# Fetching the first layer's slot tiles up to 22 ahead, and moving and spacing the gathers of batches 2 to 7

## What is computed

```python
x = x + cumsum(layernorm(x) @ W.T + bias)                 # within a row of 128
x = x + ffn(layernorm(x))
x = x + attention(layernorm(x))                           # 16 heads, window of 128
x = x + ffn(layernorm(x))

def ffn(x):                                               # 8 experts, the best 2 for each token
    xn = layernorm(x) * gamma + beta
    probs = softmax(xn @ router_w.T / 1.5)
    w, idx = top_k(probs, 2)
    h = silu(einsum('btd,edf->betf', xn, W1))
    y = einsum('betf,efd->betd', h, W2)
    return sum over the 2 chosen experts of w * y, + x
```

## Time and profile before

| | us |
|---|---|
| median of 3 runs | 991.28 |
| lowest, highest | 985.68, 997.75 |
| profiled execution, its own time | 1000.25 |
| profiled execution, span of the trace | 997.8 |
| PE busy | 693.9 (70%) |
| DVE busy | 612.3 (61%) |
| POOL busy | 434.2 (44%) |
| ACT busy | 408.3 (41%) |

### The profile page before, as it was taken

The page is one execution under the profiler, slowest core; times in us unless marked ns, Lnnn a source line. Parts: engine busy times, 40 slices in busy tenths (PEclk is TensorE's granted clock), DMA queues, the critical chain, the costliest instruction groups (busy, mean ns, idle before and its releaser), DMA issues.

```text
span 997.8 us, 30496 instructions
## 1 busy us (share of the span) xinstructions
PE 693.9 (70%) x11616; PEld 531.7 (53%) x11616; DVE 612.3 (61%) x1840; ACT 408.3 (41%) x691; POOL 434.2 (44%) x409
## 2 busy tenths in 40 slices
PE   3701767797667678887977888877586677566670
PEld 2501556675556554654645656655475556455560
DVE  7887887864444567555646655677669534354444
ACT  1370245353333334553735645645354334233340
POOL 6691573584655500203023000050576666665661
PEclk9655678999877799998999989957658988788986
DMA  7200012132212221111111201001021111233114
GB/s 220 68 27 5 23 35 70 47 68 57 62 51 82 71 78 33 55 60 29 58 46 51 60 20 42 6 15 31 17 67 39 43 44 38 64 84 97 54 37 136
DMA packets 62922, 54.60 MB, mean 55 GB/s; under 512 B 10129, under 2 KB 55954, under 8 KB 62778
## 3 DMA queue, kind: packets, MB, share of 16 engines
q1 hardware_dynamic: 53250, 33.12, 11.6%
q0 software_dynamic: 9536, 19.55, 7.8%
HBM read 31.79 MB, written 20.84 MB: 53 GB/s over the span
## 4 chain that ended last, share of the span: by engine, by line
PE 40%; DVE 27%; issue 11%; another core or an unknown queue 9%; DVEq 4%; ACT 4%; DMA 2%; POOL 1%; SPq 0%; ACTq 0%; POOLq 0%
PE stbank L1107 6%; PE bank L1210 4%; PE stbank L1094 3%; PE stbank L1096 3%; DVE zr L584 3%; PE sbank L1168 3%; DVE gl L765 2%; PE stbank L1194 2%; PE stbank L1108 2%; PE sbank L1163 2%; PE stbank L1095 2%; DVE xs L781 2%; DVE mx L823 2%; DVE ysb L755 2%
## 5 line engine op out<-in xcount | busy, mean ns | idle before, releaser
L478 POOL DMA_INDIRECT xg<-table,idx x156 | 159.1, 1020 | 170.0 <-PE sbank L1075 60.6
L901 ACT ACTIVATE g<-stbank 128x512 f32<-128x512 f32 x156 | 93.3, 598 | 324.0 <-PE stbank L1096 239.7
L1107 PE MATMUL stbank<-wff,gh 128*128 x624 | 142.6, 307 | 111.3 <-DVE ysb L755 75.8
L433 POOL TENSOR_TENSOR r<-ve,mhalf 128x4 f32<-128x4 f32 (+1 forms) x32 | 43.0, 1344 | 299.1 <-DVE ve L561 201.7
L823 DVE TENSOR_REDUCE mx<-sbank 128x2 f32<-128x320 f32 (+1 forms) x256 | 116.6, 472 | 79.7 <-PE sbank L1168 59.3
L1094 PE MATMUL stbank<-xT,wff 128*128 128x128 f16 x624 | 152.1, 250 | 17.5 <-issue 8.9
L755 DVE TENSOR_REDUCE ysb<-stbank 128x128 f32<-128x256 f32 x156 | 66.0, 423 | 155.5 <-remote 101.6
L1096 PE MATMUL stbank<-xT,wff 128*128 128x128 f16 x624 | 152.1, 250 | 0.5 <-issue 0.5
L1095 PE MATMUL stbank<-xT,wff 128*128 128x128 f16 x624 | 149.9, 247 | 1.1 <-issue 1.1
L948 ACT ACTIVATE pT<-stbank 128x1024 f32<-128x1024 f32 (+1 forms) x128 | 117.0, 915 | 76.8 <-PE stbank L1194 76.0
L1107 PEld LDWEIGHTS stbank<-wff,gh 128*128 128x128 f16 x624 | 67.5, 108 | 143.9 <-issue 126.5
(11 more groups left out here) (188 smaller groups left out, 1344.1 us busy)
## 6 DMA issues: line engine op xcount, KB each, us to landing
yslot<-ysb SPq DMA_DIRECT2D x78, 64.0 KB
table<-tb SPq DMA_DIRECT2D x16, 256.0 KB
cg<-ytab SPq DMA_DIRECT2D x16, 256.0 KB
qz<-dumps SPq DMA_DIRECT2D x96, 32.0 KB
kst<-dumps SPq DMA_DIRECT2D x96, 32.0 KB
xg<-table,idx POOLq DMA_INDIRECT x156
xs<-in_x SPq DMA_DIRECT2D x8, 256.0 KB, 4.6
qz<-in_w SPq DMA_DIRECT2D x1, 2048.0 KB, 10.2
```

Of the source, the lines that this page charges most:

```text
L478: g.indirect_dma_start(xg[:, i % G].rearrange("p a d -> p (a d)"), None, table[cc % 2], bass.IndirectOffsetOnAxis(ap=idx[:, cc % 2, t:t + ...
L901: a.activation(g32[:, i % 3, :], hbank[i % 2], ACT.Silu, scale=1.0 / WSCALE)
L1107: mm(o, gh[:, i % 3, P * f:P * f + P], whl, start=(f == 0), stop=False, skip_group_check=True)
```

## The change

In layer 0 the slot tiles are fetched into a ring of 24 in the memory of `pT`, up to 22 tiles ahead, by a table of how many are issued by each step (`x_issued`): in chunk 0 four in step 0, and then one and a half for each step, up to 39; from step 24 on the first 22 tiles of chunk 1, five in four steps; the last 17 tiles of chunk 1 in its steps 14 to 25, one and a half for each step. A tile waits for the transpose of the tile 24 before it. Each pair of ring places has a semaphore. Layer 1 is as before.

Of the results that are brought back, batches 0 and 1 stay where they were. Batch 2 is fetched in the prologue, with a wait for each on DVE's maxima (`s_red`), batch 3 and the rest of the batches in attention, each with a wait on the exponentials (`s_e`) of the unit in which it stands. `combine` of batches 2 and 3 moves to the prologue and to batch 0 of attention, as it already was for batches 4 to 7.

```diff
+RING = 24
+RING_LEAD = RING - 2
+IDX_STEP = 24
+HOLD_STEPS = 14
+BACK_EARLY = 2
+        xring = pT[:].rearrange("p a n -> p (a n)").bitcast(F16).rearrange("p (i a d) -> p i a d", a=2, d=D)
+        def x_landed(i):
+
+            first = tile_of(CHUNKS, 0)
+            if i < first:
+                return s_gp[i % RING // 2], 32 * (i // RING + 1)
+            return s_g[(i - first) % G], 16 * ((i - first) // G + 1)
+
+        def x_issued(cc, s):
+
+            if cc >= CHUNKS:
+                return min(tile_of(cc, s + AHEAD + 1), tile_of(cc + 1, 0))
+            if cc == 0 and s < IDX_STEP:
+                return min(AHEAD + 1 + s + (s + 1) // 2, SLOT_TILES)
+            if cc == 0:
+                return min(SLOT_TILES + (s - IDX_STEP + 1) * 5 // 4, SLOT_TILES + RING_LEAD)
+            return min(SLOT_TILES + RING_LEAD + max(s - HOLD_STEPS + 1, 0) * 3 // 2, 2 * SLOT_TILES)
@@
-            return s - BACK_AT if 0 <= s - BACK_AT < BPC * GATHERS else None
+            return s - BACK_AT if 0 <= s - BACK_AT < BACK_EARLY * GATHERS else None
@@
-                for t in range(AHEAD + 1) if s == 0 else (s + AHEAD,):
-                    if t < SLOT_TILES:
-                        i = tile_of(cc, t)
-                        wait(pool, s_xp, i - G + 1)
+                for i in range(x_issued_before(cc, s), x_issued(cc, s)):
+                    c, t = i // SLOT_TILES, i % SLOT_TILES
+                    wait(pool, s_xp, i - (RING if c < CHUNKS else G) + 1)
@@
+            for m in range(GATHERS):
+                wait(pool, s_red, 2 * m)
+                gather_back(2, m)
             front(2, 2)
+            for m in range(2):
+                gather_back(3, m)
             for b in range(B):
                 for j in range(UNITS):
-                    if BPC <= b + 4 < B and j in (UNITS - 3, UNITS - 1):
+                    if BACK_EARLY <= b + 4 < B and j in (UNITS - 3, UNITS - 1):
+                        wait(pool, s_e, UNITS * b + j)
                         gather_back(b + 4, (j - (UNITS - 3)) // 2)
-                    if BPC <= b + 3 < B and j % 2 == 0 and j // 2 + 2 < GATHERS:
+                    if BACK_EARLY <= b + 3 < B and j % 2 == 0 and j // 2 + 2 < GATHERS:
+                        wait(pool, s_e, UNITS * b + j)
                         gather_back(b + 3, j // 2 + 2)
@@
-                if j in (MAX_AT, UNITS - 1):
-                    front(2, 2 if j == MAX_AT else 3)
+                if j >= MAX_AT:
+                    front(2, j - MAX_AT)
```

More of the change, by code:

```diff
@@ L162, in build @@
         s_idx = sem("slot_indices_ready")
-        s_g = [sem(f"gathered{i}") for i in range(G)]; s_xp = sem("x_transposed"); s_xt = sem("xt_ready")
+        s_g = [sem(f"gathered{i}") for i in range(G)]; s_gp = [sem(f"pair_gathered{i}") for i in range(RING // 2)]; s_xp = sem("x_transposed"); s_xt = sem("xt_ready")
         s_h = sem("h_psum"); s_gh = sem("g_ready"); s_gl = sem("g_low_ready"); s_y = sem("y_psum"); s_yc = sem("y_copied")
@@ L206, in tile_of, with x_tile, x_issued_before @@
             return SLOT_TILES * cc + t
+        def x_tile(i):
+            first = tile_of(CHUNKS, 0)
+            return xring[:, i % RING] if i < first else xg[:, (i - first) % G]
+        def x_landed(i):
+            first = tile_of(CHUNKS, 0)
+            if i < first:
[9 more added lines that the diff above has]
+            return min(SLOT_TILES + RING_LEAD + max(s - HOLD_STEPS + 1, 0) * 3 // 2, 2 * SLOT_TILES)
+        def x_issued_before(cc, s):
+            if s:
+                return x_issued(cc, s - 1)
+            return x_issued(cc - 1, XSTEPS - 1) if cc else 0
         def scattered(slot, end):
@@ L225, in combined_at @@
             b = s - BACK_AT - GATHERS - 1
-            return b // GATHERS if b >= 0 and b % GATHERS == 0 and b // GATHERS < BPC else None
+            return b // GATHERS if b >= 0 and b % GATHERS == 0 and b // GATHERS < BACK_EARLY else None
         def prepared_at(s):
@@ L469, in x_step @@
                     g.memset(z.bitcast(F32), 0.0).then_inc(s_zero, 1)
-                if s == 0:
-                    pool.wait_ge(s_idx, cc + 1)
-                    for i in range(2):
-                        pool.wait_ge(s_tbd[i], 16 * 2 * (cc + 1))
-                for t in range(AHEAD + 1) if s == 0 else (s + AHEAD,):
-                    if t < SLOT_TILES:
-                        i = tile_of(cc, t)
-                        wait(pool, s_xp, i - G + 1)
-                        g.indirect_dma_start(xg[:, i % G].rearrange("p a d -> p (a d)"), None, table[cc % 2],
-                                             bass.IndirectOffsetOnAxis(ap=idx[:, cc % 2, t:t + 1], axis=0)).then_inc(s_g[i % G], 16)
+                for i in range(x_issued_before(cc, s), x_issued(cc, s)):
+                    c, t = i // SLOT_TILES, i % SLOT_TILES
+                    if t == 0:
+                        pool.wait_ge(s_idx, c + 1)
+                        for k in range(2):
+                            pool.wait_ge(s_tbd[k], 16 * 2 * (c + 1))
+                    wait(pool, s_xp, i - (RING if c < CHUNKS else G) + 1)
+                    g.indirect_dma_start(x_tile(i).rearrange("p a d -> p (a d)"), None, table[c % 2],
+                                         bass.IndirectOffsetOnAxis(ap=idx[:, c % 2, t:t + 1], axis=0)).then_inc(x_landed(i)[0], 16)
                 for t in (s - 6,) if s < XSTEPS - 1 else (s - 6, s - 5):
@@ L788, in front @@
                 if j in (0, 1):
-                    if b >= BPC:
+                    if b >= BACK_EARLY:
                         combine(0, b, j)
@@ L1071, in x_step @@
                     i = tile_of(cc, s)
-                    pe.wait_ge(s_g[i % G], 16 * (i // G + 1))
+                    pe.wait_ge(*x_landed(i))
                     wait(pe, s_xt, i - 1)
                     for a2 in range(2):
-                        ins = pe.transpose(xbank[i % 2][:, P * a2:P * a2 + P], xg[:, i % G, a2, :], ident16[:])
+                        ins = pe.transpose(xbank[i % 2][:, P * a2:P * a2 + P], x_tile(i)[:, a2, :], ident16[:])
                     ins.then_inc(s_xp, 1)
```

## The result

The changed kernel takes 1019.5 us against 993.7 for the kernel before (medians of four runs each on one chip; the kernel before has one run more than in the table above, hence 993.7 for 991.3): ratio 1.027, 95% interval 1.017 to 1.036. It is slower by 26 us, where 974, 17 us less than before, had been forecast.

A forecast was written before the change was run, and what follows sets the result against it. No engine is full; PE's signals are held back while POOL issues indirect DMAs close together. Terms 1 + 5 + 1 - 18 - 11 + 5 = -17 us, set on the median 991.3, gave 974, range 950 to 1003.

The forecast's parts named there:

- the rate inside a long run: Fetch runs beyond their first 7 us: a tile takes 6.6 us in place of 3.3, read from a run of eight.
- item 2: Chunk 0, 150 to 191: 21 fetches follow, about 17 at once; about 2 tiles lost, +5 us (0 to 14).
- item 3: Chunk 0, 191 to 232: nine fetches in a row at its end, +2, PE's waits gone; sum +1 us (0 to 4).
- item 4: Chunk 1: present holds of 38 us go, runs of 17 and 16 fetches lose 17; -18 us (-30 to 0).
- item 6: Batches 2 and 3, moved to prologue and attention: combine, later statistics and a hold of up to 2; +5 us (3 to 8).
- Item 1: Chunk 0, steps 0 to 9: five more fetches between POOL's powers, mostly hidden in idle time; +1 us (0 to 6).
- item 5: Attention, batches 4 to 7: spaced fetches remove DVE's 13.4 us of waits; -11 us (-13.4 to -6).
- Rival S: Runs of 17, 17 and 16 fetches in chunks 0 and 1: holds start at once, over 80% held; +17, 1008 us, chance 0.16.
- B: Fetch runs throughout: holds last to the end of a run and nothing passes; sum 0, 991 us, chance 0.19.
- A: The main forecast: first 7 us of a run harmless, tiles then pass slowly; 974 us (965 to 985), chance 0.40.
- Rival N: POOL is not the cause, "remote" waits stay and fetch order changes nothing; 995 to 997 us, chance 0.08.
- the signs named: Changed profile: fetch runs of 17 to 21, tick distance in them, chunk 1 and prologue times, no DVE "remote" wait in attention.

The follow-up runs named there:

- the microkernel: A kernel without the computation: PE and ACT exchange ticks beside POOL's series of fetches; 0.58 us a tick undisturbed, mostly 2.80 us apart when held.

## Why the prediction was wrong

The mechanism was read rightly and the size of one term, the rate inside a long run, was wrong; it stands in the items 2 to 4. The prologue (item 6) was mis-sized as well.

- Item 1, +1: tile 7 comes 1.7 us later, but DVE waited 1.55 us for a late signal just before it, so that this belongs to item 2; on the free chip tile 7 comes at 158.3, as before the change.
- Item 2, +5 (0 to 14): +14.5. The step that failed: "The first 7 us do no harm (as in attention); in the other 14 a tile takes 6.6 us by rows 6". The first half was about right, if anything too kind: a signal of 156.74, 7 us into the run, was late. The rate was wrong: behind the first 7 us one tick came, at 159.92, and the next 17.0 us later; for 14.8 us not even a signal passed. In two of the other three held profiles of the changed kernel the tick of tile 7 itself came only at 174.5 and 174.6. The 6.6 us were never a rate. In the earlier trace rows the tick at 286.52, itself after a wait of 1.94 us for "remote", is the last that got through and that at 293.13 the first behind the run; I took the two ends of one stop for two tiles passing through it.
- Item 3, +1: +8.6. The run of nine (234.36 to 245.59) was expected to be held for 4 us; ticks stand at 239.38 and then 247.33, behind the run. The same step.
- Item 4, -18 (-30 to 0): -2.0. Against the free chips, chunk 1 loses 31 us to holds before (135.9 against 105.0), and not 38, and 34 after (133.9 against 100.3), where 17 were expected. The run without the ring shows -14.5 for the moved fetches alone, so the ring took 12.5 us back. The same step again.
- Item 5, -11: -10.8 in the batches 1 to 4. The right size.
- Item 6, +5 (3 to 8): +15.8. On the free chip the same edit costs 3 to 6 us, near the forecast. The rest is only there where signals are held: the prologue takes 25.8 us against 18.3, at the lower clock, and without its fetches 16.7. The term "with a hold of up to 2: +1" again counted 7 harmless us; a signal was 2 us late within the first microsecond (PE's score of 394.39, the first fetch at 393.58). What the late signals cost by themselves and what the lower clock that goes with PE's gaps is not separated.

Rival S had the mechanism and its places: item 2 at +17 (14.5), item 3 at +5 (8.6), item 4 at 0 (-2.0). Its 1008 falls short by item 6. What seemed to speak against it and B was the tick at 286.52; by the earlier trace rows, where each hold ends 1.1 to 1.8 us behind a run, B and S should have had more than A. Of the signs named, stretches of 14 us and more without a tick in the runs of 17 and 19 (B or S), chunk 1 at 134 (S: 136) and no "remote" wait of DVE in attention (item 5) came out.

Rival N, which was also what the rule in the Trainium skill, "SBUF — State Buffer", section "Who interferes with whom", would give (PE never waits on anyone), is wrong on a held chip: PE's signals wait for POOL's fetches in a kernel with nothing else in it. That section is about access to SBUF, and as such the traces don't contradict it: PE's matmul starts 0.25 us after ACT's and what is late is the news of it. Applying it to signals was the error. On a free chip N describes the runs. The Trainium skill's "Perfetto Trace Analysis", section "Per-instruction lifecycle: what the profiler-reported window actually captures", says that the propagation of a semaphore lies outside the window that the profile reports. The traces agree: PE's row ends at 32.62, and 2.3 us pass until ACT starts, of which only "remote" in ACT's row tells.

## What to carry to other kernels

Before fetching further ahead, ask what still paces the fetches: four buffers that wait for PE were also what kept POOL's indirect DMAs in runs of four, and a deeper ring took that away. Where an engine's wait ends at "remote" shortly behind a run of POOL's indirect DMAs, take the two ticks around it as the two ends of a stop, not as a rate, and spread the fetches over work (a wait for a later unit, or something else for POOL to do) rather than clearing for clearing's sake, which costs where POOL is close to the bound. A tuning that cures this on one chip may be worth nothing on the next: measure on more than one.

## What the hardware showed that was not expected

- The kernel before takes 911 us on some chips and 991 to 998 on others, 8 to 9% apart, at the same instructions. In the stages: chunk 1 105 against 136 us, layer 1 253 against 282 to 289, attention (spaced on the free chips) 300 to 303 against 322.
- On the held chips, in the microkernel, signals of PE and DVE come out in multiples of 0.7 us once POOL's indirect DMAs have been 1.16 to 1.25 us apart for 12 to 19 us, and until up to 9.7 us behind them; ACT's signals (0.25 us) are not held. Fetches of 32 rows do it as those of 128 do; 16 ordinary DMAs from POOL's queue, over in 8.5 us, did not.
- In the kernel a hold starts sooner. In chunk 1 runs of four, each just behind another, are enough; in chunk 0 signals are late 7 us into the run, and in the prologue at once, 0.8 us after a fetch that follows the last one by 30 us. What fills up and drains is not shown by any run here, nor what distinguishes the chips.
